# Table stage of a graph network: GpSimd normalises the vector features and adds the self connection

## The reference, cut to what matters

```
x = x + ffn0(layernorm(x))            # the second block: sum of two picked experts, normalised
n = layernorm(x)                      # per node, over all 256 features
x0, x1 = n[:, :64], n[:, 64:].reshape(-1, 64, 3)
s0, s1 = x0 @ sc_w0 * a / 8,  einsum('nuc,uv->nvc', x1, sc_w1) * a / 8      # self connection
y0, y1 = x0 @ lin1_w0 * a / 8, einsum('nuc,uv->nvc', x1, lin1_w1) * a / 8   # table that the messages gather
x = x + c_s * (s0, s1) + c_x * (messages made of y)
```

## Time and profile before

| | |
|---|---|
| median of three runs | 2060.71 us |
| span of the profiled execution | 2058.3 us |
| TensorE busy | 1788.4 us (87%) |
| VectorE busy | 1128.1 us (55%) |
| ScalarE busy | 1009.7 us (49%) |
| GpSimd busy | 1075.1 us (52%) |
| mean granted TensorE clock | 0.925 |

### The profile page before, as it was taken

The page is one execution under the profiler, slowest core; times in us unless marked ns, Lnnn a source line. Parts: engine busy times, 40 slices in busy tenths (PEclk is TensorE's granted clock), DMA queues, the critical chain, the costliest instruction groups (busy, mean ns, idle before and its releaser), DMA issues. The chain is left out here.

```text
span 2058.3 us, 38371 instructions
## 1 busy us (share of the span) xinstructions
PE 1788.4 (87%) x9937; PEld 1447.4 (70%) x9937; DVE 1128.1 (55%) x2765; ACT 1009.7 (49%) x3031; POOL 1075.1 (52%) x1464
## 2 busy tenths in 40 slices
PE   2699999999779867999936599999999998997899
PEld 1456565655446656999924589899889887775788
DVE  6333333333322375554456799999999993333122
ACT  4344444444214523333236677777777764553222
POOL 2688888888820003555400788888888850000443
PEclk7799999999889757999967899999999999997899
DMA  9677777776650025666562777777777771555553
GB/s 236 187 227 237 237 225 228 237 238 218 205 183 16 21 65 170 208 214 215 190 144 67 229 213 216 215 215 217 214 216 216 216 192 43 174 164 147 172 180 121
DMA packets 226048, 377.06 MB, mean 183 GB/s; under 512 B 65641, under 2 KB 113202, under 8 KB 225600
## 3 DMA queue, kind: packets, MB, share of 16 engines
q1 hardware_dynamic: 171436, 220.22, 35.2%
q0 software_dynamic: 52224, 150.15, 24.7%
q10 hardware_dynamic: 2190, 4.34, 0.8%
HBM read 275.59 MB, written 100.00 MB: 182 GB/s over the span
## 5 line engine op out<-in xcount | busy, mean ns | idle before, releaser
L1801 POOL DMA_INDIRECT msg_got<-y_dram,block_src x416 | 418.1, 1005 | 198.1 <-POOLq L78 100.4
L661 POOL DMA_INDIRECT ffn_w<-xn_dram,block_src x416 | 394.9, 949 | 109.7 <-issue 94.4
L1822 ACT ACTIVATE msg_scaled<-msg_plain,msg_w 128x125 f32<-128x125 f32 x1044 | 311.9, 386 | 96.2 <-DVE msg_plain L1854 95.2
L710 PEld LDWEIGHTS sum_ps_sum<-ffn_w,sum_onehot 128*125 128x125 f32 x928 | 170.9, 194 | 200.4 <-issue 184.4
L710 PE MATMUL sum_ps_sum<-ffn_w,sum_onehot 128*125 x928 | 258.2, 403 | 44.8 <-POOLq L655 43.4
L770 DVE TENSOR_TENSOR agg<-sum_ps_sum,agg 125x256 f32 x232 | 98.5, 425 | 316.6 <-PE sum_ps_sum L710 316.2
L741 ACT ACTIVATE sum_wide<-sum_ps_w,sum_rec 128x128 f32<-128x128 f32 x416 | 129.9, 363 | 236.4 <-PE sum_ps_w L695 236.4
L695 PE MATMUL sum_ps_w<-sum_fc,sum_hid 128*128 128x512 f32 x416 | 212.7, 593 | 0.0
L1843 PEld LDWEIGHTS msg_ps_z<-msg_prod,msg_scaled 128*125 128x125 f32 x1416 | 173.9, 188 | 6.7
L1843 PE MATMUL msg_ps_z<-msg_prod,msg_scaled 128*125 128x128 f32 x1416 | 174.5, 273 | 0.0
L1883 DVE TENSOR_TENSOR agg<-msg_ps_z,agg 125x512 f32 x232 | 159.4, 687 | 20.6 <-DVE agg L1883 1.3
(11 more groups left out here) (353 smaller groups left out, 3194.3 us busy)
## 6 DMA issues: line engine op xcount, KB each, us to landing
edge_w<-sum_wide SPq DMA_DIRECT2D x52, 1040.0 KB, 5.4
msg_w<-edge_w SPq DMA_DIRECT2D x174, 260.0 KB
ffn_run_w<-in_L_ffn_w SPq DMA_DIRECT2D x64, 512.0 KB
x_sb<-edge_w SPq DMA_DIRECT2D x58, 260.0 KB
ffn_rows<-agg SPq DMA_DIRECT2D x25, 448.0 KB
ffn_w<-in_L_ffn_w SPq DMA_DIRECT2D x16, 512.0 KB, 8.7
wd<-in_L_ffn_Wd SPq DMA_DIRECT2D x8, 1024.0 KB
ffn_w<-xn_dram,block_src POOLq DMA_INDIRECT x416, 3.7
```

The source lines that it names most:

```text
L661: pool.indirect_dma_start(got[:, (b + 1) % RING, u, :], None, k.xn_dram, bass.IndirectOffsetOnAxis(ap=k.block_src[:, b, u:u + 1].bitcast(U ...
L710: last = pe.matmul(ps_sum[n % ZB][0:P, :], onehot[n % OB][:, u, :], got[:, ds(need % RING, 1), u, :].rearrange("p o d -> p (o d)"), start= ...
L1801: pool.indirect_dma_start(got[:, (b + 1) % RING, u, :, :].rearrange("p k v -> p (k v)"), None, k.y_dram, bass.IndirectOffsetOnAxis(ap=k.bl ...
L1822: last = act.activation(scaled[s % MB][:, x, c, :], plain[s % MB][:, c, :], ACT.Copy, scale=w[s % RS][:, c, D + x:D + x + 1])
```

## The change

Two pieces of work go to GpSimd. `normalise_vectors` does what L1664 did on ScalarE, five operations a group. `add_self` moves there from VectorE, its vector part split in three operations, one for each component. ScalarE keeps the scalars. The signal `xs_made` becomes two, `scalars_made` and `vectors_made`, and TensorE's `turn` waits for both.

```diff
@@ -1534,8 +1534,8 @@
         got_in, w_made = ph.sems("got_in", NG), ph.sem("w_made")
         z_made, z_counted, z_mv_done, z_std_done, z_rstd_done, u_made, x_made = (
             ph.sem(x) for x in ("z_made", "z_counted", "z_mv_done", "z_std_done", "z_rstd_done", "u_made", "x_made"))
-        x_counted, x_mv_done, x_std_done, x_rstd_done, shift_done, xs_made = (
-            ph.sem(x) for x in ("x_counted", "x_mv_done", "x_std_done", "x_rstd_done", "shift_done", "xs_made"))
+        x_counted, x_mv_done, x_std_done, x_rstd_done, shift_done, scalars_made, vectors_made = (
+            ph.sem(x) for x in ("x_counted", "x_mv_done", "x_std_done", "x_rstd_done", "shift_done", "scalars_made", "vectors_made"))
         turned, kept, made, y_made, added = (ph.sem(x) for x in ("turned", "kept", "made", "y_made", "added"))
         stored = ph.sems("stored", 2)
         block = ph.ctx.enter_context(nc.Block())
@@ -1608,19 +1608,13 @@
             def x_root(i):
                 dve.wait_ge(x_std_done, i + 1)
                 if i >= 2:
-                    dve.wait_ge(xs_made, 2 * G * (i - 1))
+                    dve.wait_ge(scalars_made, G * (i - 1))
+                    dve.wait_ge(vectors_made, G * (i - 1))
                 dve.reciprocal(x_rstd[0:P, i % 2, :], x_std[0:P, :]).then_inc(x_rstd_done, 1)
                 dve.wait_ge(x_rstd_done, i + 1)
                 dve.wait_ge(x_mv_done, G * (i + 1))
                 dve.scalar_tensor_tensor(x_shift[0:P, i % 2, :], x_mv[0:P, :, 0], -1.0, x_rstd[0:P, i % 2, :], ALU.mult, ALU.mult)\
                    .then_inc(shift_done, 1)
-
-            def add_self(i):
-                x, own = k.x_sb[0:P, i * G:i * G + G, :], ys[i % 2][0:P, :, 1, :]
-                x_vectors = x[:, :, MUL:D].rearrange("p j (u c) -> p j c u", c=3)
-                dve.wait_ge(y_made, G * (i + 1))
-                dve.tensor_tensor(x[:, :, 0:MUL], own[:, :, 0:MUL], x[:, :, 0:MUL], ALU.add).then_inc(added, 1)
-                dve.tensor_tensor(x_vectors, own[:, :, MUL:D].rearrange("p j (c u) -> p j c u", c=3), x_vectors, ALU.add).then_inc(added, 1)
 
             dve.wait_ge(m.raw_in, 128)
             for which, factor in enumerate((INV_MUL, INV_MUL * C_S)):
@@ -1633,10 +1627,32 @@
                 if i + 1 < NG:
                     sum_picks(i + 1)
                 x_root(i)
+                if i + 1 < NG:
+                    z_root(i + 1)
+
+        @block.gpsimd
+        def _(pool):
+            def normalise_vectors(i):
+                pool.wait_ge(shift_done, i + 1)
+                if i >= 2:
+                    pool.wait_ge(turned, G * (i - 1))
+                for j in range(G):
+                    pool.tensor_scalar(xs[i % 2][0:P, j, MUL:D].rearrange("p (c u) -> p c u", c=3), vectors_apart(k.x_sb[0:P, i * G + j, :]),
+                                       x_rstd[0:P, i % 2, j:j + 1], x_shift[0:P, i % 2, j:j + 1], ALU.mult, ALU.add).then_inc(vectors_made, 1)
+
+            def add_self(i):
+                x, own = k.x_sb[0:P, i * G:i * G + G, :], ys[i % 2][0:P, :, 1, :]
+                x_vectors = x[:, :, MUL:D].rearrange("p j (u c) -> p j c u", c=3)
+                pool.wait_ge(y_made, G * (i + 1))
+                pool.tensor_tensor(x[:, :, 0:MUL], own[:, :, 0:MUL], x[:, :, 0:MUL], ALU.add).then_inc(added, 1)
+                for c in range(3):
+                    last = pool.tensor_tensor(x_vectors[:, :, c, :], own[:, :, MUL + c * MUL:2 * MUL + c * MUL], x_vectors[:, :, c, :], ALU.add)
+                last.then_inc(added, 1)
+
+            for i in range(NG):
+                normalise_vectors(i)
                 if i >= 1:
                     add_self(i - 1)
-                if i + 1 < NG:
-                    z_root(i + 1)
             add_self(NG - 1)
 
         @block.scalar
@@ -1660,9 +1676,7 @@
                 for j in range(G):
                     x, to = k.x_sb[0:P, i * G + j, :], xs[i % 2][0:P, j, :]
                     shift, rstd = x_shift[0:P, i % 2, j:j + 1], x_rstd[0:P, i % 2, j:j + 1]
-                    act.activation(to[:, 0:MUL], x[:, 0:MUL], ACT.Identity, bias=shift, scale=rstd).then_inc(xs_made, 1)
-                    act.activation(to[:, MUL:D].rearrange("p (c u) -> p c u", c=3), vectors_apart(x), ACT.Identity, bias=shift, scale=rstd)\
-                       .then_inc(xs_made, 1)
+                    act.activation(to[:, 0:MUL], x[:, 0:MUL], ACT.Identity, bias=shift, scale=rstd).then_inc(scalars_made, 1)
 
             def keep(t):
                 act.wait_ge(turned, t + 1)
@@ -1696,7 +1710,8 @@
         @block.tensor
         def _(pe):
             def turn(t):
-                pe.wait_ge(xs_made, 2 * t + 2)
+                pe.wait_ge(scalars_made, t + 1)
+                pe.wait_ge(vectors_made, t + 1)
                 if t >= TB:
                     pe.wait_ge(kept, t - TB + 1)
                 for q in range(2):
```

## The result

Four runs of the changed kernel have a median of 2043.62 us (2042.24 to 2049.1), four of the kernel before 2061.14. The ratio is **0.9929 [0.9906, 0.9951]**, so the change makes the kernel faster by 0.7%. That is more than the 0.5% that can be told from no change, to which the prediction gave a chance of 0.22. The profiled execution has a span of 2047.3 us (before: 2058.3).

What follows compares the result with a forecast made beforehand. ScalarE and TensorE, one chain at 13.7 us a group, were taken as the bound. The stage's -6.1 and its end's +1.6 gave -4.5: span 2053.8, plus 2.4 to the median, 2056 us; range 2046 to 2070.

Steps and rivals of the forecast that it cites:

- -6.1 + 1.6 = -4.5: Stage from group 0's shift: 62.4 us to the last scale against 68.5, then 1.6 more at its end.
- ScalarE's queue, 2.6 us a group: ScalarE loses five operations a group, so TensorE's first product starts about 2.1 instead of 4.74 us after the group began.
- Turns on a shared port: VectorE's two-input operations and GpSimd's SBUF reads want one port pair; one stands until the other is through.
- Nine GpSimd operations against ten of `add_norm`, one by one: Each period GpSimd and VectorE alternate singly, holding VectorE 4.4 us together; chance 0.5 as the main forecast.
- Group 4, 10.9 long: Last group: VectorE idle, vectors undisturbed, so it takes 13.49 - 2.6 = 10.9 us.
- End of the stage, +1.6: After the last product, GpSimd's final add_self and its store issues take 6.3 us instead of 4.7.
- GpSimd's prices: GpSimd in the stage: 0.31 us per vector operation, 3.94 for add_self; low 0.165 and 2.2, high 0.54 and 6.8.
- twice my price: Sign that the forecast is wrong: GpSimd operations in the stage taking twice the forecast price.
- hardly any blocking: Rival: turns not taken or GpSimd operations at the low end, ScalarE and TensorE bound; 2049 or 2048 us, chance 0.2.
- keep the port through its run of ten: Rival: add_norm runs without a gap, GpSimd's vectors start 4.1 us late, first product at 5.9; 2058 us, chance 0.15.
- the 18.5 of that rival: Rival: GpSimd at its high prices makes VectorE the bound, with a period of 18.5 us; 2072 us, chance 0.15.

Runs made afterwards that it cites:

- vectors_only: The changed kernel with add_self left on VectorE, so GpSimd only normalises the vectors: 2045.20 us, ratio 0.9952 to the kernel before.
- self_only: The changed kernel with ScalarE normalising everything as before, so GpSimd only does add_self: 2056.34 us, ratio 1.0003 to the kernel before.
- write_only: The changed kernel with GpSimd setting the vector features to zero instead of normalising them: 2045.1 us in one run.
- late_self: The changed kernel with GpSimd's add_self begun only when add_norm of the next group is done: 2042.64 us, ratio 0.9930 to the kernel before.
- gamma_psum: The changed kernel with gamma copied to PSUM once, so five operations of add_norm read one SBUF input: 2041.31 us, ratio 0.9933 to the kernel before.

## Where the prediction held and where it failed

It had the sign and the source of the gain, and missed the size: it took the wrong number of turns on the shared port, the wrong clock for the last group, and too long an end. Its sum for the stage was -6.1 + 1.6 = -4.5, the trace has -12.0. Point by point:

- *ScalarE's queue, 2.6 us a group:* right in kind, and vectors_only and self_only show that the gain is there. The first product came at 2.07 in two groups and at 3.45 in three, since a vector operation beside `add_norm` lasts 0.98: 9.2 us in five groups, not 5 x 2.6 = 13.0.
- *Turns on a shared port:* right that there are turns; the ten operations are slower only where GpSimd reads. Not right that one stands until the other is through, as the prediction and the page quoted in it have it: a vector operation and two products one behind the other would need 0.58 + 2 x 0.39 = 1.36 us, and 0.98 was measured, so they overlap. Of the pairs that the prediction read, L317 beside L431 was a fill, which only writes; write_only shows that a fill does not hold the products, so that only L426 was like the case.
- *Nine GpSimd operations against ten of `add_norm`, one by one:* **the step that failed.** It gave VectorE a hold of 1.0 from the vectors and 3.5 from `add_self` in each period. The 1.0 came out, from two errors that cancel: the operation is twice as long (0.58 for 0.31), but two products pass for one. The 3.5 did not: five vectors already fill the ten products, and the additions come after them. Measured are 0 in groups 3 and 4 (but for 0.57 under one sum, L1571) and 1.9 in group 2. The shifts are 10.93, 13.51, 11.49 and 10.53 us apart, where 11.1, 14.5, 14.5 and 11.4 were forecast. Group 4 starts at 48.1 instead of 51.5 after the first shift: 3.4 of the missed 7.5 us. (Group 3 starts 4.1 earlier than in the sum, 36.0 against 40.1, and takes 12.15 instead of 11.4.)
- *Group 4, 10.9 long:* 8.28. The forecast left TensorE's clock where the earlier trace rows have it. The group's six transposes now follow without a gap, 1.11 us after TensorE's products of group 3, and the clock stayed at 1.00, also in both further profiles of the change. This is 2.6 of the 7.5, and the forecast did not consider it. The shorter wait alone does not bring it: late_self has the same wait and the same head at .83 and 9.95, and in write_only the last group, with its first product at 2.07, took 10.68 at .68, nearly the forecast. What decides between them stays open.
- *End of the stage, +1.6:* +0.1. GpSimd's last additions end at 1124.28 + 2.76 = 1127.04, 3.65 after the last `scale`, and SyncE's last issue ends 1.16 after that, where 4.4 and 1.9 were allowed. This is 1.5 of the 7.5.
- *GpSimd's prices:* `add_self` 3.6 (forecast 3.94), the vector operation 0.58 (0.31, high end 0.54: too low, and near the "twice my price" that was named as a sign of being wrong). As the products passed two by two, the longer operation helped VectorE.
- *The rivals:* "hardly any blocking" gave nearly the time (2048 to 2049), and by the wrong way: blocking there is, in every period. VectorE does not keep the port through its run of ten (0.98 a turn), and GpSimd was above the high end for the vectors without a period near the 18.5 of that rival.

Why two products pass one operation of 0.58 and only one an addition of 0.94 is not settled. The rows would fit a GpSimd operation that needs the port for a part of its time only, and asks for it late enough to let a second product in; no run measured that part, and none separated the length of the operation from its number of inputs.

## What to carry to other kernels

When two engines share a port, don't count turns: look at one pair in the trace, since an operation of 0.58 us with one input and one of 0.94 with two took turns at different ratios here, and ask which later operation is pushed out of the conflict by an earlier one. A conflict of two-input operations can be taken away by an operand in PSUM, without moving any work (gamma_psum). Moved work that begins when the other engine is at operations with one input does not hold that engine there (late_self: 4.69 for 6.77), but look at what it then meets: here it was the next sum, and the stage gained nothing that can be told apart. When a wait before a matmul becomes shorter, price the matmuls behind it at both of the clock's levels: the same last group took 8.28 us at 1.00 and 9.95 at .83.

## What was not expected of the hardware

- A GpSimd operation with one SBUF input beside two-input operations of VectorE: 0.98 us instead of 0.58, and VectorE loses 0.2 for each; an addition: 1.11 instead of 0.94, and VectorE loses 0.65.
- A fill by GpSimd of 192 elements a partition takes 0.2 us (1.05 for five) and costs VectorE's products beside it nothing (3.92 for ten).
- A step of three floats in a GpSimd read and no step in its write cost 0.1 us in 0.58.
- TensorE held the granted clock of 1.00 through a whole group of 8.28 us in all three profiles of the change, and its first four products fell from 2.07 to 1.13 us; behind the same wait of 1.11 us it was .83 in late_self.
